# A graph network's second layer: the last three stores of a pass as single transfers of 125 partitions

## The chip, the cores and the metric

The kernel runs on one core of a Trainium2 chip. The metric is the time of the whole program in microseconds of device time, the median of several executions. TensorE (PE) multiplies matrices into PSUM banks, VectorE (DVE), ScalarE (ACT) and GpSimd (POOL) work elementwise, and SyncE (SP) issues most of the transfers between the on-chip memory (SBUF) and the device memory. The transfers themselves are carried out by 16 DMA engines.

## What is computed

Four graph layers follow one another on a table of 10,000 nodes with 512 features; each adds its result to its input and normalises every row. The change touches the second layer only, a fixed-point iteration over 2,500 edges sorted by target:

```
step(out):  Ax  = segment_sum(sup[:, None] * out[edge_col], edge_row)
            out = (x * b + (Ax + out) * a) / denom
x = layernorm(x + scan(step, x, length=10))
```

An edge has a weight `sup`, a source `edge_col` and a target `edge_row`. Each of the ten iterations needs the rows of the previous one at every edge's source.

## The kernel before

Nodes without an edge need no iteration, so the kernel keeps only one row per edge in sorted order: `E` = 2,500 rows in `ET` = 20 tiles of `P` = 125 rows (one row of 512 floats, 2,048 bytes, per partition). A target whose edges lie in two neighbouring tiles has its row in one of `NM` = 20 extra shared rows, `EM`. The values of the iteration lie in the SBUF tile `Y[125, 20, 512]` (in the first pass in `CR`).

The ten iterations are written as a first one without a table and nine passes i = 1 to 9 of the same shape. A pass goes through a table in device memory, because every edge needs the row of an arbitrary other edge:

- SP (`sp_L1`, lines 1195 to 1206) writes `Y` to the table `Yd[i % 2]` (`y_table` in the trace). `Y_STORES` (line 1396) cuts the 20 tiles into seven stores: tiles 0-3, 4-7, 8-11, 12-15, then 16-17, 18 and 19. Each waits on the semaphore `P_out` for its last tile. `store_tiles` (line 1182) makes two transfers of a store: one of the partitions 0 to 111 (`HI` = 112, line 1185) and one of the 13 partitions 112 to 124 (line 1186). After the seven stores the shared rows follow, one transfer of 20 rows (line 1201), once DVE has them (`M_rows`).
- All 15 transfers of a pass raise one semaphore, `y_put`. `Y_PUT` (line 1397) is what a pass adds to it.
- POOL (`pool_L1`) waits until `y_put` holds everything of the pass (line 1422) and then issues 20 indirect transfers, one per tile, that gather the rows into `V1` (line 1424).
- PE (`pe_L1`) multiplies each gathered tile t with the tile's weights `Ss` into bank t mod 5 (line 1473, waits for gather t), and once per four tiles adds to the sums of the shared rows (line 1438). After the last tile it forms the shared rows (line 1491).
- DVE (`dve_L1`, line 1633) turns bank t into `Y[:, t, :]` and raises `P_out`; at the end it makes the shared rows (line 1642, raises `M_rows`). ACT (line 1525) writes the constant part of the next pass into the bank that came free.

So one pass is a ring: gathers, products, rows, stores, and then the next pass's gathers, which may read any row and therefore wait for all the stores. The order of the stores on SP's queue is the order of the code.

Of the kernel before, what the change touches and what calls it, by code (L numbers as in the profile page):

```python
# [5 lines left out]
P = 125  # L6
# [35 lines left out]
def gnn_kernel(nc, x, x_cols, cols, rows, b1_row, wsmall, w32, w_ffn, w_left, ident_in, w_r1, w_r2, w_l1, w_l2, w_q, w_k, w_v, w_o,  # L42
               keys, key_cols, rec_in, earlier_in, mask_in, abs_in, out):
    ctx = ExitStack()
    with ctx:
# [3 lines left out]
        def sem(name):  # L49
            return ctx.enter_context(nc.semaphore(name))  # L50
# [13 lines left out]
        def at(off, shape, parts=128, dt=F32):  # L64

            n = 1
            for v in shape:
                n *= v
            assert off + n <= AR, (off, shape)
            ap = arena[0:parts, off:off + n]  # L70
            if dt != F32:
                ap = ap.bitcast(dt)
            if len(shape) == 2:
                ap = ap.rearrange("p (a b) -> p a b", b=shape[1])
            return ap
# [650 lines left out]
        Yd = [nc.dram_tensor(f"y_table{q}", (E + NM, D), F32).ap() for q in range(2)]  # L726
# [216 lines left out]
        def store(sp, table, base, g, rows4, s):  # L943

            dst = grp(table[base:base + E, :], g)
            sp.dma_start(dst[0:HI], rows4[0:HI]).then_inc(s, 16)
            sp.dma_start(dst[HI:P], rows4[HI:P]).then_inc(s, 16)

        def load(sp, rows4, table, base, g, s):
            src = grp(table[base:base + E, :], g)  # L950
            sp.dma_start(rows4[0:HI], src[0:HI]).then_inc(s.s, 16)
            sp.dma_start(rows4[HI:P], src[HI:P]).then_inc(s.s, 16)
# [229 lines left out]
        def store_tiles(sp, table, t0, t1, rows, s):  # L1182

            dst = table[t0 * P:t1 * P, :].rearrange("(t p) d -> p t d", p=P)
            sp.dma_start(dst[0:HI], rows[0:HI, t0:t1, :]).then_inc(s, 16)
            sp.dma_start(dst[HI:P], rows[HI:P, t0:t1, :]).then_inc(s, 16)

        def sp_L1(sp, c):
            for g in range(EG):
                c.y += TG  # L1190
                sp.wait_ge(L_y, c.y)
                store_tiles(sp, X1s, g * TG, (g + 1) * TG, Y, x1s_put)
            sp.dma_start(EM[:, :], Y[P - 1:P, :, :]).then_inc(m_in, 16)

            def step(i, par):
                first = isinstance(i, int) and i == 1
                for t0, t1 in Y_STORES:
                    sp.wait_ge(P_out, t1 if first else i * ET + (t1 - ET))
                    store_tiles(sp, Yd[par], t0, t1, CR if first else Y, y_put)
                sp.wait_ge(M_rows, i)  # L1200
                sp.dma_start(Yd[par][E:E + NM, :], EM[:, :]).then_inc(y_put, 16)
            step(1, 1)
            with sp.Fori(1, ITERS // 2) as h:
                step(h * 2, 0)
                step(h * 2 + 1, 1)
            for g in range(EG):
                sp.wait_ge(P_cr, ET * (ITERS - 2) + TG * (g + 1))
                if g == 0:
                    sp.wait_ge(x1s_put, 32 * EG)
                load(sp, CR[:, g * TG:(g + 1) * TG, :], X1s, 0, g, e1_f[g])  # L1210
            sp.wait_ge(*e1_f[EG - 1].full(32))
            for g in range(EG):
                sp.wait_ge(*e1_f[g].full(32))
            sp.wait_ge(M_rows, ITERS)
            sp.dma_start(CRM[:, :], CR[P - 1:P, :, :]).then_inc(m_in, 16)
            sp.wait_ge(P_out, ET * ITERS)
            for dst, src in ((WQ, w_q), (WK, w_k), (WV, w_v), (WO, w_o)):
                sp.dma_start(dst, src).then_inc(w2_in, 16)
            for g in range(EG):
                c.y += TG  # L1220
                sp.wait_ge(L_y, c.y)
                store(sp, X2d, 0, g, Y[:, g * TG:(g + 1) * TG, :], x2_put)
            sp.wait_ge(xm_rdy, 1)
            sp.dma_start(X2d[2 * E:2 * E + NM, :], EM[:, :]).then_inc(x2_put, 16)
            sp.wait_ge(x2_put, X2_ALL)
# [142 lines left out]
        V1, Y, CR = at(6312, [ET, D], P), at(16552, [ET, D], P), at(26792, [ET, D], P)  # L1368
# [3 lines left out]
        y_put = sem("y_put")  # L1372
# [21 lines left out]
        x1s_put, m_in = sem("x1_by_src_put"), sem("shared_rows_in")  # L1394
        m_pre, xm_rdy, m_sc, m_rt = sem("shared_before_sums"), sem("shared_x2"), sem("shared_var"), sem("shared_root")
        Y_STORES = [(0, 4), (4, 8), (8, 12), (12, 16), (16, 18), (18, 19), (19, 20)]
        Y_PUT = 32 * len(Y_STORES) + 16
        X2_ALL = 2 * 32 * EG + 16
        RING1 = 5

        def pool_L1(pool, c):
# [19 lines left out]
            for i in range(1, ITERS):  # L1421
                pool.wait_ge(y_put, i * Y_PUT)
                for t in range(ET):
# [110 lines left out]
        def dve_L1(dve, c):  # L1534
# [90 lines left out]
            def step(i):  # L1625
                dve.wait_ge(y_put, i * Y_PUT)
                nc.vector.scalar_tensor_tensor(EM, EM, RRM[:, 0:1], CRM, ALU.mult, ALU.add).then_inc(m_pre, 1)

                before = CR if isinstance(i, int) and i == 1 else Y

                def own(t):
                    dve.wait_ge(P_sum, i * ET + (t + 1))
                    nc.vector.scalar_tensor_tensor(Y[:, t, :], before[:, t, :], RR[:, t:t + 1], bank[t % RING1][0:P, :],  # L1633
                                                   ALU.mult, ALU.add).then_inc(P_out, 1)
                for t in range(ET - 1):
                    own(t)
                dve.wait_ge(M_ps, i + 1)
                nc.vector.tensor_copy(MB, bank[7][:, :]).then_inc(M_sb, 1)
                own(ET - 1)
                dve.wait_ge(m_pre, i)  # L1640
                dve.wait_ge(M_ps2, i + 1)
                nc.vector.scalar_tensor_tensor(EM, bank[5][0:NM, :], RRM[:, 0:1], EM, ALU.mult,
                                               ALU.add).then_inc(M_rows, 1)
# [1107 lines left out]
```

## Time and profile before

| | us |
|---|---|
| Median of 3 runs (3117.52 to 3121.24) | 3119.29 |
| The profiled execution's own time | 3123.35 |
| Its span, first to last instruction | 3121.5 |
| Idle time of POOL that the stores' landing ended, over 9 passes | 110.5 |
| First and last gather issue of the nine passes (`y_table`), from the span's start | 1624.2 and 2003.7 |

The span is one execution as the hardware profiler saw it. An engine's busy time says little by itself here; what counts is which wait ends last at each turn of the ring. SP's transfers appear in a timeline at the moment SP issues them, with the time the issue took; when the data moves is seen in the share of time for which the 16 DMA engines carry packets, where one engine that is always busy counts 1/16 = 0.06. A transfer's landing is seen in who waited for it.

### The profile page before, as it was taken

To read this page: it belongs to the slowest core of one execution; us is meant where nothing else is said; L and a number is where in the kernel's file an instruction comes from. 1 tells how busy PE (TensorE), PEld (TensorE's weight loads), DVE (VectorE), ACT (ScalarE), POOL (GpSimd) and SP (SyncE) were. 2 spreads that over 40 slices of the span, in tenths; PEclk is the share of its full clock that TensorE was granted. 3 is DMA by queue.
4 is the path that set the end of the run, shared out by engine and by line. 5 is a ranking of instruction groups with operands and counts; after the bars stand their busy time and mean duration, and the time that the engine had idled before them with its cause. 6 is when DMAs were issued, how large, how long until landed. Compare 5 with 4: busy or idle time off the path is not lost.

```text
span 3121.5 us, 29317 instructions
## 1 busy us (share of the span) xinstructions
PE 2388.7 (77%) x9340; PEld 1248.1 (40%) x9340; DVE 1899.9 (61%) x3792; ACT 1300.8 (42%) x1935; POOL 1164.3 (37%) x850
## 2 busy tenths in 40 slices
PE   5779999999998448987066766539888777568877
PEld 2445555555555324543021111124443643235455
DVE  3378989889899741235753434545556547737663
ACT  2898888888874311120422322201110012145544
POOL 1354553644648434310625565420220202133322
PEclk8899999999999679999578878769888588779989
DMA  6224333333332144316725545740120101132212
GB/s 200 79 71 119 96 102 117 96 114 108 103 114 73 43 120 136 91 56 184 198 82 153 159 124 151 192 123 0 54 60 18 40 18 48 40 86 69 71 45 56
DMA packets 212498, 297.37 MB, mean 95 GB/s; under 512 B 98571, under 2 KB 98941, under 8 KB 210998
## 3 DMA queue, kind: packets, MB, share of 16 engines
q1 hardware_dynamic: 107436, 213.12, 22.8%
q0 software_dynamic: 104960, 82.99, 10.6%
q8 instruction: 53, 0.87, 0.1%
q14 instruction: 49, 0.39, 0.0%
HBM read 170.88 MB, written 160.48 MB: 106 GB/s over the span
## 4 chain that ended last, share of the span: by engine, by line
PE 39%; DVE 21%; issue 11%; ACT 10%; POOL 9%; DMA 7%; SPq 2%; DVEq 0%; POOLq 0%; ACTq 0%
PE bank L1823 7%; PE bank L847 6%; POOL arena L939 5%; POOL arena L1424 5%; ACT RD L414 3%; PE bank L2249 3%; DVE st L525 3%; PE bank L827 2%; PE bank L289 2%; DMA arena<-y_table,ids 2%; PE bank L290 2%; ACT arena L855 2%; PE bank L2132 2%; ACT arena L467 2%; PE bank L801 1%
## 5 line engine op out<-in xcount | busy, mean ns | idle before, releaser
L939 POOL DMA_INDIRECT arena<-x_table,idd x120 | 156.3, 1303 | 697.7 <-DVE arena L905 317.9
L282 PE MATMUL bank<-arena 128*125 128x512 f32 x640 | 290.4, 608 | 41.0 <-DMA arena<-x_cols 23.1
L847 PE MATMUL bank<-arena 128*125 128x512 f32 x640 | 283.5, 601 | 8.9 <-DVE arena L1343 7.0
L1424 POOL DMA_INDIRECT arena<-y_table,ids x180 | 229.1, 1273 | 162.6 <-DMA y_table<-arena 110.5
L298 PE MATMUL bank<-arena 128*125 128x512 f32 x640 | 278.8, 593 | 1.3 <-ACT arena L391 1.3
L659 POOL TENSOR_TENSOR arena<-arena,rowv 125x512 f32<-125x512 f32 x80 | 106.8, 1367 | 461.7 <-PE bank L290 167.1
L1473 PE MATMUL bank<-arena 125*125 125x512 f32 x360 | 206.2, 705 | 91.5 <-DMA arena<-y_table,ids 88.5
L1633 DVE SCALAR_TENSOR_TENSOR arena<-arena,v,bank 125x512 f32<-125x512 f32 x180 | 134.5, 747 | 202.3 <-PE bank L1473 193.8
L855 ACT ACTIVATE arena<-bank 128x500 f32<-128x500 f32 (+1 forms) x210 | 116.5, 590 | 322.9 <-PE bank L827 233.2
L1525 ACT ACTIVATE bank<-arena 125x512 f32<-125x512 f32 x180 | 107.9, 601 | 283.3 <-DVE arena L1633 278.3
L801 PE MATMUL bank<-ident,arena 125*128 125x125 f32 x640 | 101.8, 326 | 158.6 <-DMA arena<-x_table,idd 106.3
L1823 PE MATMUL bank<-arena 128*125 128x512 f32 x480 | 213.8, 608 | 3.8 <-ACT arena L855 3.8
L861 ACT ACTIVATE lsr<-lsr 125x4 f32<-125x4 f32 (+1 forms) x55 | 11.2, 204 | 480.6 <-DVE lsr L894 448.6
L282 PEld LDWEIGHTS bank<-arena 128*125 128x125 f32 x640 | 119.9, 192 | 197.0 <-issue 171.7
L847 PEld LDWEIGHTS bank<-arena 128*125 128x125 f32 x640 | 120.4, 191 | 161.1 <-issue 149.8
L298 PEld LDWEIGHTS bank<-arena 128*125 128x125 f32 x640 | 120.2, 188 | 154.2 <-issue 154.0
L801 PEld LDWEIGHTS bank<-ident,arena 125*128 125x128 f32 x640 | 93.6, 186 | 181.0 <-issue 104.5
L855 ACT ACTIVATE arena<-bank,colv 128x500 f32<-128x500 f32 (+1 forms) x105 | 70.6, 709 | 220.4 <-PE bank L801 129.9
L1473 PEld LDWEIGHTS bank<-arena 125*125 125x125 f32 x360 | 68.0, 213 | 230.5 <-issue 173.7
L661 POOL TENSOR_SCALAR arena<-arena,q 125x512 f32<-125x512 f32 x80 | 159.2, 2003 | 0.0
L391 ACT ACTIVATE arena<-bank,colv 128x500 f32<-128x500 f32 x220 | 139.5, 713 | 35.8 <-PE bank L290 34.6
L274 PE MATMUL bank<-ident,arena 125*128 125x125 f32 x960 | 125.2, 286 | 36.3 <-ACT arena L476 28.1
(390 smaller groups left out, 4997.7 us busy)
## 6 DMA issues: line engine op xcount, KB each, us to landing
y_table<-arena SPq DMA_DIRECT2D x36, 896.0 KB
p_table<-arena SPq DMA_DIRECT2D x25, 896.0 KB
z_table<-arena SPq DMA_DIRECT2D x25, 896.0 KB
x_table<-arena SPq DMA_DIRECT2D x25, 896.0 KB
arena<-x_cols SPq DMA_DIRECT2D x20, 1000.0 KB, 6.1
arena<-x SPq DMA_DIRECT2D x20, 896.0 KB
out<-arena SPq DMA_DIRECT2D x20, 896.0 KB
x_by_src<-arena SPq DMA_DIRECT2D x5, 896.0 KB
```

Of the source, the lines that this page charges most:

```text
L282: i = nc.tensor.matmul(b[0:P, :], xT[:, k, j * P:(j + 1) * P], W1r[:, k, :], start=k == 0, stop=k == KC - 1)
L298: i = nc.tensor.matmul(b[0:P, :], hT[:, k, j * P:(j + 1) * P], W2r[:, k, :], start=k == 0, stop=k == KC - 1)
L391: nc.scalar.activation(dst, st_.bank(part, i)[0:parts, 0:GR], func, **kw).then_inc(NT_sb, 1)
L661: nc.gpsimd.tensor_scalar(T[1 - par][:, j, :], T[1 - par][:, j, :], q2[1 - par][:, j:j + 1], None, ALU.mult).then_inc(B["wq"], 1)
L801: i = nc.tensor.transpose(b[:, j * P:(j + 1) * P], src, ident[0:P, 0:P])
L847: i = nc.tensor.matmul(b[0:P, 0:n], fT[:, k, j * P:(j + 1) * P], W[:, k, :], start=q * KC + k == 0, stop=q * KC + k == last)
L855: nc.scalar.activation(dst, bank[(c.t - 1) % 4][0:src_rows, 0:n], func, **kw).then_inc(T_sb, 1)
L939: nc.gpsimd.indirect_dma_start(out=dst, out_offset=None, in_=table, in_offset=bass.IndirectOffsetOnAxis(ap=idx, axis=0), bounds_check=limi ...
L1424: nc.gpsimd.indirect_dma_start(out=V1[0:P, t, :], out_offset=None, in_=Yd[i % 2], in_offset=bass.IndirectOffsetOnAxis(ap=ids[:, 2, t:t + 1 ...
L1473: nc.tensor.matmul(bank[t % RING1][0:P, :], Ss[:, t, :], V1[:, t, :], start=False, stop=True, skip_group_check=True).then_inc(P_sum, 1)
L1633: nc.vector.scalar_tensor_tensor(Y[:, t, :], before[:, t, :], RR[:, t:t + 1], bank[t % RING1][0:P, :], ALU.mult, ALU.add).then_inc(P_out, 1)
L1823: i = nc.tensor.matmul(b[0:P, :], fT[:, k, j * P:(j + 1) * P], W[:, k, :], start=k == 0, stop=k == KC - 1)
```

## The change

The first four stores of a pass stay pairs of 112 and 13 partitions. The last three (tiles 16-17, tile 18, tile 19) become one transfer of all 125 partitions each, issued from line 1203 of the changed kernel. The sum that `y_put` reaches in a pass is adapted: 12 transfers instead of 15.

```diff
-                    store_tiles(sp, Yd[par], t0, t1, CR if first else Y, y_put)
+                    rows = CR if first else Y
+                    if t1 - t0 > 2:
+                        store_tiles(sp, Yd[par], t0, t1, rows, y_put)
+                    else:
+                        sp.dma_start(Yd[par][t0 * P:t1 * P, :].rearrange("(t p) d -> p t d", p=P),
+                                     rows[0:P, t0:t1, :]).then_inc(y_put, 16)
...
-        Y_PUT = 32 * len(Y_STORES) + 16
+        Y_PUT = sum(32 if t1 - t0 > 2 else 16 for t0, t1 in Y_STORES) + 16
```

On SP's queue the end of a pass in the loop reads as follows before the change; `y_table` is the table, `arena` the SBUF region that holds `Y` and the shared rows, and the sizes are partitions x (tiles x) elements:

```order
L1185 DMA y_table<-arena 112x2x512
L1186 DMA y_table<-arena 13x2x512
L1198 REGISTER_ALU
L1185 DMA y_table<-arena 112x512
L1186 DMA y_table<-arena 13x512
L1185 DMA y_table<-arena 112x512
L1186 DMA y_table<-arena 13x512
L1201 DMA y_table<-arena 20x512
```

And so after it:

```order
L1203 DMA y_table<-arena 125x2x512
L1198 REGISTER_ALU
L1203 DMA y_table<-arena 125x512 x2
L1206 DMA y_table<-arena 20x512
```

Three transfers of 13 partitions are gone from each pass, nothing changes place, and the other engines' instructions are the same.

## Rows read from the trace of the kernel before

**Rows 1.** The chain that ended last, from 1620 to 2010 us, by line:
```profile
by line: POOL arena L1424 36.2%; issue 30.2%; DMA arena<-y_table,ids 15.7%; PE bank L1473 5.6%; DMA y_table<-arena 4.3%; PE bank L1438 3.0%; PE bank L1491 1.7%; DVE arena L1642 1.2%; POOLq L1424 0.9%; SPq L1186 0.5%; SPq L1185 0.5%; DVE are
```

**Rows 2.** A wait of POOL, 1620 to 2010 us: total us, times, longest us:
```profile
POOL arena L1424 <- DMA y_table<-arena: 110.5, 9, 15.2
```

**Rows 3.** Last chain again, single pieces (start, us, what), four of nine:
```profile
1621.81 1.47 DMA y_table<-arena
...
1753.44 1.51 DMA y_table<-arena
...
1927.95 1.77 DMA y_table<-arena
...
1970.02 2.83 DMA y_table<-arena
```

**Rows 4.** Timeline, end of pass 8 (start, us, engine, line, operation):
```profile
1920.22 0.31 SPq L1185 DMA_DIRECT2D y_table<-arena  x1
...
1924.02 0.31 SPq L1185 DMA_DIRECT2D y_table<-arena  x1
...
1926.92 0.31 SPq L1185 DMA_DIRECT2D y_table<-arena  x1
...
1927.95 0.27 SPq L1201 DMA_DIRECT2D y_table<-arena  x1
...
1930.62 1.27 POOL L1424 DMA_INDIRECT arena<-y_table,ids  x1 [10.97 <-DMA y_table<-arena]
```

**Rows 5.** Timeline of SP, loads of 125 partitions at the program's start:
```profile
30.64 0.57 SPq L2544 DMA_DIRECT2D Sd<-keys  x1
31.26 4.60 SPq L2544 DMA_DIRECT2D Md<-keys  x1
```

**Rows 6.** Windows while these loads run; last two columns DMA share and GB/s:
```profile
24.00:28.00 4.00, 3.31 (x19) 2.00 (x19) 0.00 (x0) 1.51 (x3) 0.00 (x0) 1.00 1.06 214
...
36.00:40.00 4.00, 4.00 (x11) 1.70 (x10) 1.88 (x3) 0.00 (x0) 2.76 (x3) 1.00 0.32 117
40.00:44.00 4.00, 3.58 (x9) 1.29 (x7) 1.00 (x2) 0.00 (x0) 1.52 (x2) 1.00 0.33 132
```

**Rows 7.** Windows in passes 5, 2 and 8: length, engines busy, PEclk, DMA share, GB/s:
```profile
1800.00:1800.50 0.50, 0.00 (x0) 0.00 (x0) 0.00 (x0) 0.00 (x0) 0.00 (x0) 1.00 0.00 0
1800.50:1801.00 0.50, 0.00 (x0) 0.00 (x0) 0.00 (x0) 0.00 (x0) 0.00 (x0) 1.00 0.35 82
...
1660.00:1661.00 1.00, 1.00 (x9) 0.29 (x2) 0.72 (x2) 0.74 (x2) 0.00 (x0) 1.00 0.91 260
...
1921.00:1931.00 10.00, 4.99 (x16) 1.24 (x16) 4.47 (x7) 2.40 (x4) 0.39 (x1) 1.00 0.67 216
```

**Rows 8.** The page's DMA queue of SP (packets, MB, share of 16 engines):
```profile
q1 hardware_dynamic: 107436, 213.12, 22.8%
```

**Rows 9.** Timeline of SP, shared rows' store in pass 5:
```profile
1799.90 0.27 SPq L1201 DMA_DIRECT2D y_table<-arena  x1
```

**Rows 10.** Timeline of SP, end of pass 4, the stores of tiles 16-17 and 19:
```profile
1745.58 0.31 SPq L1185 DMA_DIRECT2D y_table<-arena  x1
...
1752.41 0.31 SPq L1185 DMA_DIRECT2D y_table<-arena  x1
```

**Rows 11.** Timeline of SP, store of tiles 16-17 in pass 1:
```profile
1615.51 0.30 SPq L1185 DMA_DIRECT2D y_table<-arena  x1
```

**Rows 12.** Timeline, end of pass 6, from the store of tiles 16-17 on:
```profile
1837.60 2.12 SPq L1186 DMA_DIRECT2D y_table<-arena  x1
...
1841.17 0.74 DVE L1642 SCALAR_TENSOR_TENSOR arena<-bank,arena 20x512 f32<-20x512 f32 x1 [0.29 <-PE bank L1491]
...
1842.61 0.33 SPq L1201 DMA_DIRECT2D y_table<-arena  x1
```

**Rows 13.** Last chain, end of pass 8: the piece of the last gathers:
```profile
1915.21 6.75 DMA arena<-y_table,ids
```

## The prediction, made before the changed kernel ran

> **What bounds the kernel now.** I read first the chain that ended last, cut to the stretch of the second layer's loop. It is made of the gathers' issues on POOL and the pauses between them, then of the landing of the last gathers, the last products, and the landing of the stores [rows 1]. PE, the busiest engine of the page, is a guest here. Then the waits of POOL: its only real wait in the loop is for the stores of `y_table`, nine times, once a pass, 110.5 us in all [rows 2]. So a pass is: 20 gathers issued one after the other, the last one lands, the last rows are made, the last stores land, the next pass begins. Whatever moves the moment at which all stores of a pass have landed moves everything behind it by the same amount, nine times; no other work can hide it, since every gather waits for it.
>
> The third view is that moment itself. The chain's pieces show how long the last transfer (the 20 shared rows) took from issue to landing: 1.47 to 1.51 us in passes 1, 3, 4 and 5, and 1.76 to 2.83 us in passes 2, 6, 7, 8 and 9 [rows 3]. The first group finds an idle queue; in the second the transfer stands behind stores that are still being carried out. In pass 8 it was issued at 1927.95 and landed at 1929.7, and the next pass's first gather began at 1930.62 [rows 4]. So in five passes of nine the DMA engines are already the last thing to finish, and the question is what the change does to the queue in front of them.
>
> **The change, part by part.** (1) *Removed:* three issues of 13 partitions a pass on SP. (2) *Changed:* three transfers of 112 partitions become transfers of 125. The bytes are the same: 250, 125 and 125 rows of 2,048 bytes.
>
> What the second part costs depends on how many DMA engines a transfer of 125 partitions uses. No such store is in the trace, but loads of that shape are: from 31 us on SP has only transfers of 125 partitions under way [rows 5], and the DMA share falls from 1.06 to a plateau of 0.32 to 0.33 [rows 6]. 5/16 is 0.31. I read that as five engines busy and eleven idle. Stores cut at 112 reach a share of 0.91 [rows 7], all sixteen.
>
> The Trainium skill says the same from the other side ("DMA: Bandwidth & Descriptors", section "Why a DMA increments its semaphore by 16 and not by 1"): a transfer takes the largest number of engines up to 16 that divides its slowest dimension, which makes 16 of 112, 13 of 13 and 5 of 125; and on this path they are the lowest-numbered ones. The plateau agrees. The same page's section "Rules for kernel authors" speaks for the change: two transfers to disjoint halves of the partitions are no use, one should take a single transfer. By that rule the sum would be the second rival's.
>
> So per engine: before, a tile is 7 rows on each of 16 engines and one more on 13 of them, 8 at most. Now it is 25 rows on each of five. The three stores put 2x8 + 8 + 8 = 32 rows on an engine before and 50 + 25 + 25 = 100 after.
>
> *Time of a row.* Loads on five engines: 132 GB/s at a share of 0.33, 25 GB/s an engine, 0.082 us for 2,048 bytes [rows 6]. Stores on sixteen, beside gathers: 260 GB/s at 0.91, 17.9 GB/s an engine, 0.115 us [rows 7]. The average of SP's queue over the program is 0.228 x 16 x 3121.5 / 107436 = 0.106 us a packet [rows 8]. The new stores run on five engines, like the loads, but they are stores of shorter rows (the loads bring 2,500 numbers to a partition), partly beside gathers. I take **0.095 us**, a little nearer to the loads, and keep 0.082 and 0.115 as ends.
>
> *Start and landing.* The shared rows of pass 5 were issued at 1799.90 into an idle queue [rows 9]; up to 1800.5 nothing moved, then all did [rows 7]. I take 0.85 us from issue to first row. With 1.47 us in all for a similar one [rows 3] and 2 rows an engine, 0.4 us remain for the landing.
>
> *A pass with a full queue (pass 8)* [rows 4]. Tiles 12-15 are issued at 1920.22; 28 + 4 rows an engine at 0.106 us after 0.85 us end at 1924.5. Tiles 16-17 are issued at 1924.02, so data starts at 1924.9, and 50 rows last until 1929.6. Tile 18 (issued by then) ends at 1932.0, tile 19 at 1934.4, the shared rows at 1934.6, landed at 1935.0. Before it was 1927.95 + 1.77 = 1929.72. **+5.2 us**, and 26 for the five passes of this kind.
>
> *A pass in which tile 19 comes late (pass 4)* [rows 10]. Tiles 16-17 start at 1746.4, end at 1751.2; tile 18 ends at 1753.6; tile 19, issued at 1752.41, stands behind it and ends at 1755.9; shared rows landed at 1756.5, against 1753.44 + 1.51 = 1754.95. +1.6. The same working gives +1.3 for pass 3 and +0.5 for pass 5, where the gap in front of tile 19 is longest: 3.4 together.
>
> *Pass 1* stores one after the other what lies ready, with 6.3 us from the issue of tiles 16-17 to that of the shared rows [rows 3, 11]: 1616.4 + 102 x 0.095 + 0.4 = 1626.5, against 1623.3. +3.2.
>
> *The removed issues* are worth something only where SP is late. The shared rows are ready at 1841.91 in pass 6 and issued at 1842.61, 0.7 us late, because SP had stood 2.12 us at a 13-partition transfer [rows 12]; pass 9 looks the same, with the longest landing of all, 2.83 us [rows 3]. That gain is counted at nothing: the transfer that would be issued sooner then waits behind 100 rows on its engines. I also count nothing for the wait of SP at the larger transfers: it stood 4.6 us at them at the start [rows 5], but only while their engines had work queued, and those engines set the end.
>
> **Sum:** 26 + 3.4 + 3.2 = 32.6 us. Against the profiled execution (3123.35 us, of which 3121.5 span) that is 3156.0; that execution is 4.1 us above the median of the runs, so the forecast for the median is 3119.3 + 32.6 = **3152 us**. With 0.082 us a row a full pass costs 5.2 - 102 x 0.013 = 3.9 us, pass 1 costs 1.9 and the three others some 1 together, 22 us in all; with 0.115 it is 7.2 x 5 + 5.2 + 9 = 50 us. That gives 3141 to 3169.
>
> **The rivals.**
> - *Five engines, but not always the same five.* If each transfer took other engines, the 100 rows would not queue on one. Tile 19 of pass 8 would end at 1926.92 + 0.85 + 2.4 = 1930.2, landed at 1930.6, +0.9; nine times that is 8 us: 3127. For it: the plateau of 0.32 shows one share, not which engines. Against: consecutive loads on different engines would overlap and lift the share over 0.31, and it stayed there for 8 us [rows 6].
> - *The other side: 125 partitions spread evenly.* Then each transfer is as fast as the pair, 8 rows an engine, and SP has three issues less. SP's stop of 2.12 us in pass 6 [rows 12], and the like in pass 9, shrinks, which brings tiles 18 and 19 out up to 1.5 us earlier there and 0.3 us in the three other full passes: -4 us, 3115. It decides if the new transfers' share in a pass's tail is near that of before. Against it stands the plateau, unless it came from the loads' other side, keys that all partitions read alike. To come out over 6.2 us faster, it would also have to bring the last gathers in sooner.
> - *More than the queue.* The last gathers already take 6.75 us to land [rows 13], and some of their rows share the five loaded engines, now for 5 us a pass instead of 2; and PE stands idle longer, so its granted clock, 1.00 (2.4 GHz) in those windows of pass 5 [rows 7], may be 1.2 GHz for more of the products. One to two microseconds a pass, +12: 3164.
>
> **How the numbers follow.** Forecast 0.66, more than the queue 0.13, not the same five 0.11, spread evenly 0.10. The range is to hold the first two, and the ends of the row time: down to 3135, a little under the 3141 of the cheapest row, because the drain of tiles 12-15 may be shorter than taken, and up to 3171. A run can tell 0.2%, 6.2 us, from no change. Slower by more than that are the first three cases, 0.89 with a little of the third falling under it; same 0.09; faster 0.03.
>
> **What would show it.** In the tail of a full pass the DMA share falls from 0.67 over ten us [rows 7] to some 0.4, and to 0.3 once only the new transfers are left, for about 5 us after SP's last issue. The chain's piece from the shared rows' issue to the landing grows from 1.8 to some 7 us in passes 2, 6, 7, 8 and 9, and to 2 to 3 us in 3 to 5. POOL's nine waits grow from 110.5 to some 143 us; its 180 issues and the gathers keep their durations. I am wrong if the share in the tail stays near 0.7 (spread evenly), or if it is 0.6 for half the time (different engines), or if POOL's wait grows by clearly less than the total.

## The result

| | before | changed |
|---|---|---|
| Median of 4 runs, us | 3120.26 | 3178.17 |
| Lowest and highest | 3117.52, 3127.41 | 3166.11, 3187.08 |
| Span of the profiled execution | 3121.5 | 3185.3 |

The changed kernel takes 1.0189 times as long, interval 1.0164 to 1.0214: 58 us more. The direction was as forecast; the forecast of 3152 us was 26 us too low and the time lies 7 us above the range of 3135 to 3171. One execution of an experiment's kernel (tiles 12 to 17 as one store) took 5021.87 us; it counts as slow and is left out of that run's ratio.

### The profile page after: what moved, and what is told of

The parts are those of the page before. It is cut to its first block, busy times and chain, and to the rows that moved or that the text cites. A ratio compares the mean times of both kernels' runs of the same rounds, so it can differ in the third digit from the quotient of the medians.

```text
span 3185.3 us, 29290 instructions
## 1 busy us (share of the span) xinstructions
PE 2394.6 (75%) x9340; PEld 1252.1 (39%) x9340; DVE 1900.7 (60%) x3792; ACT 1301.3 (41%) x1935; POOL 1166.2 (37%) x850
## 4 chain that ended last, share of the span: by engine, by line
PE 38%; DVE 21%; issue 11%; ACT 10%; DMA 9%; POOL 9%; SPq 2%; DVEq 0%; POOLq 0%; ACTq 0%
PE bank L1828 7%; PE bank L847 6%; POOL arena L1429 4%; POOL arena L939 4%; ACT RD L414 3%; PE bank L2254 3%; DMA y_table<-arena 3%; DVE st L525 3%; PE bank L289 2%; PE bank L827 2%; DMA arena<-y_table,ids 2%; PE bank L290 2%; PE bank L2137 2%; ACT arena L855 2%; PE bank L801 2%
## 5 line engine op out<-in xcount | busy, mean ns | idle before, releaser
L1478 PE MATMUL bank<-arena 125*125 125x512 f32 x360 | 208.8, 712 | 156.2 <-DMA arena<-y_table,ids 153.7
L1429 POOL DMA_INDIRECT arena<-y_table,ids x180 | 229.6, 1275 | 224.2 <-DMA y_table<-arena 172.1
```

The source lines that it names most:

```text
L1429: nc.gpsimd.indirect_dma_start(out=V1[0:P, t, :], out_offset=None, in_=Yd[i % 2], in_offset=bass.IndirectOffsetOnAxis(ap=ids[:, 2, t:t + 1 ...
L1478: nc.tensor.matmul(bank[t % RING1][0:P, :], Ss[:, t, :], V1[:, t, :], start=False, stop=True, skip_group_check=True).then_inc(P_sum, 1)
```

## The profile after

Lines are renumbered: the gathers are at line 1429, the stores of 125 partitions at 1203, the shared rows at 1206. POOL's wait, from 1620 to 2100 us (us in total, times, longest), answers [rows 2]:

```profile
POOL arena L1429 <- DMA y_table<-arena: 172.1, 9, 21.0
POOL arena L1429 <- issue: 52.1, 171, 0.3
```

The wait for the stores grew from 110.5 to 172.1 us, by 61.6 of the 63.8 us that the span grew. The issues' pauses are the same 52.1. So the time went where the forecast put it. The chain that ended last shows the landings of the shared rows one by one (start of the issue, us until landed). All nine after the change:

```profile
1626.15 5.14 DMA y_table<-arena
...
1672.49 11.19 DMA y_table<-arena
...
1724.19 10.95 DMA y_table<-arena
...
1775.54 10.79 DMA y_table<-arena
...
1827.18 10.83 DMA y_table<-arena
...
1878.51 8.37 DMA y_table<-arena
...
1931.27 5.03 DMA y_table<-arena
...
1977.58 9.71 DMA y_table<-arena
...
2028.35 10.83 DMA y_table<-arena
```

And the five of the kernel before that [rows 3] leaves out, passes 2, 3, 5, 6 and 7:

```profile
1663.54 1.98 DMA y_table<-arena
...
1709.03 1.51 DMA y_table<-arena
...
1799.90 1.47 DMA y_table<-arena
...
1842.61 2.60 DMA y_table<-arena
...
1885.74 1.76 DMA y_table<-arena
```

1.5 to 2.8 us became 5 to 11 us. From one landing to the next is one pass. In the kernel before, passes 2, 6, 7, 8 and 9 take 42.2 to 43.8 us, and passes 3, 4 and 5 take 44.4 to 46.4. After the change seven passes take 48.9 to 52.4 us, and pass 7 takes 49.4. The end of pass 2 in the timeline, the counterpart of [rows 4]:

```profile
1666.18 0.31 SPq L1185 DMA_DIRECT2D y_table<-arena  x1
...
1667.90 4.54 SPq L1203 DMA_DIRECT2D y_table<-arena  x3
...
1670.03 0.75 DVE L1638 SCALAR_TENSOR_TENSOR arena<-arena,v,bank 125x512 f32<-125x512 f32 x1 [0.33 <-PE bank L1478]
...
1672.49 1.49 SPq L1206 DMA_DIRECT2D y_table<-arena  x1
1683.70 0.74 DVE L1632 SCALAR_TENSOR_TENSOR arena<-arena 20x512 f32<-20x512 f32 x1 [11.90 <-DMA y_table<-arena]
1684.58 1.28 POOL L1429 DMA_INDIRECT arena<-y_table,ids  x1 [21.02 <-DMA y_table<-arena]
```

And the DMA engines meanwhile (columns as in [rows 7]: PEclk, DMA share, GB/s last):

```profile
1667.00:1677.00 10.00, 3.96 (x15) 0.68 (x13) 3.69 (x6) 2.40 (x4) 0.00 (x0) 0.89 0.56 167
...
1671.00:1681.00 10.00, 0.00 (x0) 0.00 (x0) 0.74 (x1) 0.42 (x1) 0.00 (x0) 0.69 0.32 98
...
1672.00:1674.00 2.00, 0.00 (x0) 0.00 (x0) 0.00 (x0) 0.00 (x0) 0.00 (x0) 1.00 0.32 102
1674.00:1676.00 2.00, 0.00 (x0) 0.00 (x0) 0.00 (x0) 0.00 (x0) 0.00 (x0) 0.72 0.47 118
1676.00:1678.00 2.00, 0.00 (x0) 0.00 (x0) 0.00 (x0) 0.00 (x0) 0.00 (x0) 0.50 0.31 98
1678.00:1680.00 2.00, 0.00 (x0) 0.00 (x0) 0.00 (x0) 0.00 (x0) 0.00 (x0) 0.50 0.31 113
1680.00:1682.00 2.00, 0.00 (x0) 0.00 (x0) 0.00 (x0) 0.00 (x0) 0.00 (x0) 0.50 0.08 30
1682.00:1683.50 1.50, 0.00 (x0) 0.00 (x0) 0.00 (x0) 0.00 (x0) 0.00 (x0) 0.50 0.06 22
```

The plateau at 0.31 to 0.32 is there: five engines of sixteen, from 1672 to 1680, while no other engine of the core works. The one window at 0.47 is when the shared rows move, a transfer that uses ten engines by the divisor rule; that they go out there is read from the share alone. [rows 7] has 0.67 and 216 GB/s in pass 8 of the kernel before, in a stretch that begins 0.8 us after the issue of tiles 12-15. The stretch that begins there in this pass, from 1667, has 0.56 and 167 GB/s, and the one from 1671 has 0.32 and 98.

Two things were not in the forecast. The five engines move 98 to 113 GB/s, 20 to 23 GB/s each, where the forecast read 25 from the loads [rows 6]. And from 1680 on the share is 0.08, then 0.06, which is 1/16: one engine is alone for some 3 us, while the four others have finished. It is not slower than they are at that time. In the trace's packet records its last 25 rows of tile 19 begin at 1681.15, end at 1683.15 and start 0.080 us apart, and the two shared rows follow until 1683.32; the others had ended by 1680.59. So it stands a whole tile behind by then, and lost that time earlier in the pass. In passes 3, 4 and 5 the last engine ends 2.0 to 2.6 us after the next to last, in pass 6, the shortest of the seven long ones, 0.4 us after it.

## Experiments

All times are medians, beside the kernel before on the same chip, with the ratio to it and its interval; the chip is not the same for all experiments, so they are compared by their ratios. "Rows" are the 2,048-byte rows that the most loaded DMA engine carries in a pass's three last stores and the shared rows: 34 before, 102 in the changed kernel, by the divisor rule (see the forecast).

### Another cut of the pairs

Four kernels keep pairs and 15 transfers a pass, and move only the cut of the last three stores.

```diff
-                    store_tiles(sp, Yd[par], t0, t1, CR if first else Y, y_put)
+                    store_tiles(sp, Yd[par], t0, t1, CR if first else Y, y_put, 120 if t1 - t0 <= 2 else HI)
```

(`store_tiles` takes the cut as its last argument; 100, 115 and 124 likewise.)

**120 and 5 partitions.** 

> The last three stores of a pass are pairs again, but of 120 and 5 partitions. Queue theory (what counts is the number of rows on the most loaded DMA engine, at about 0.127 us a row, as the tails of the changed kernel's passes show: 102 rows between the drain of tiles 12-15 and the landing took some 13 us): 120 spreads over 15 engines (8 rows each), 5 over five (1 row), so 9 rows a tile instead of 8, about 4 rows a pass more: 0 to +5 us against the kernel before. Rival, size theory (any transfer of more than 112 partitions is slow, because it leaves the 16-engine split, whatever the count of engines): most of the +58 us. Rival, issue theory (a single transfer holds SP for longer than a pair, and that delays what follows): 0, as there are pairs.

3121.32 us, ratio 1.0005 (0.9982 to 1.0028). No difference. A transfer of 120 partitions, more than 112, is not slow as such: the size theory is out.

**100 and 25 partitions.** 

> The last three stores of a pass are pairs of 100 and 25 partitions. Queue theory: 100 spreads over ten engines (10 rows each) and 25 over five (5 rows), so 15 rows a tile on the most loaded engines, 62 rows in the tail of a pass instead of 34. 28 rows at 0.127 us are 3.6 us a pass, +25 to +32 us. Issue theory: pairs as before, -1 to +3 us.

3136.82 against 3119.29 us, ratio 1.0065 (1.0041 to 1.009), +20 us by the ratio. Same number of transfers, same bytes, only more rows on some engines. The queue theory has the sign; its +25 to +32 lies above the median, and the interval (+13 to +28 us) reaches its lower end.

**115 and 10 partitions.** 

> The last three stores are pairs of 115 and 10 partitions. 115 spreads over five engines (23 rows each), 10 over ten (1 row): 24 rows a tile, 98 in the tail of a pass, on the same five engines as in the changed kernel, but in 15 transfers a pass as before. Queue theory: within 5 us of the changed kernel, +50 to +58 us. Issue theory (the single transfer, not its spread, costs): like the kernel before, 0. Alignment theory (in the changed kernel one of the five engines lags because of where its 25 partitions begin): the lagging engine, alone for 2 us and more at the end of half of the passes, is gone, +35 to +45 us.

3164.65 against 3115.32 us, ratio 1.0151 (1.0117 to 1.0184), +47 us. This is the decisive run: 15 transfers in pairs as before, and most of the cost of the change, because 115 has the divisor 5 and no larger one under 16. The issue theory is out. The alignment theory expected the lagging engine to be gone; in pass 4 one engine is again alone at the end:

```profile
1771.00:1773.00 2.00, 0.00 (x0) 0.00 (x0) 0.00 (x0) 0.00 (x0) 0.00 (x0) 0.50 0.38 124
1773.00:1775.00 2.00, 0.00 (x0) 0.00 (x0) 0.00 (x0) 0.00 (x0) 0.00 (x0) 0.50 0.07 29
```

**124 and 1 partition.** 

> The last three stores are pairs of 124 and 1 partition: 124 spreads over four engines (31 rows each), 1 goes to one engine: 32 rows a tile, 130 in the tail instead of 34. Queue theory, with the 0.13 us a row and pass that the runs with 17 and 34 rows more gave: 96 x 0.13 = 12.5 us a pass in full passes, +85 to +110 us against the kernel before, clearly more than the changed kernel's +58. Issue theory: 0. Size theory (over 112 partitions is slow as such): as the changed kernel, +58.

3189.5 against 3115.32 us, ratio 1.0246 (1.0211 to 1.0281), +77 us: more than the changed kernel, as only the queue theory says, a little under its numbers. The share in pass 2's tail, after SP's last issue, is 0.26 to 0.27, four engines of sixteen:

```profile
1671.00:1673.00 2.00, 0.00 (x0) 0.00 (x0) 0.00 (x0) 0.00 (x0) 0.00 (x0) 0.64 0.27 99
1673.00:1675.00 2.00, 0.00 (x0) 0.00 (x0) 0.00 (x0) 0.00 (x0) 0.00 (x0) 0.50 0.26 102
```

### One part of the change alone

```diff
-                    if t1 - t0 > 2:
+                    if not (t0 == 19):
```

(against the changed kernel; the other two have `t0 == 16` and `t0 == 18`, and `Y_PUT` is adapted.)

**Only tile 19.** 

> Only tile 19, the last store, is one transfer of 125 partitions; tiles 16-17 and 18 stay pairs of 112 and 13. Queue theory: 17 rows more on the most loaded engines, 2.2 us in each of nine passes, whether tile 19 is late or not, since nothing comes after it but the shared rows: +15 to +20 us. Issue theory: a third of the 58 us or less, and little where SP has nothing queued; +0 to +5 us in passes in which tile 19 comes late.

3139.07 us, ratio 1.0071 (1.0046 to 1.0096), +22 us.

**Only tiles 16-17.** 

> Only tiles 16-17 go as one transfer of 125 partitions; tiles 18 and 19 stay pairs. Queue theory: 50 rows instead of 16, 34 more a pass; in a pass whose tail is full (tile 19 within 3 us of tile 18) they stand in front of what follows: 4.3 us, in a pass in which tile 19 comes 6 us late they are gone by then: about 0. With five to nine full passes +22 to +39 us. Issue theory: a third of the 58 us, +19 us, alike in all passes.

3143.99 us, ratio 1.0106 (1.0077 to 1.0135), +33 us by the ratio, +25 by the medians.

**Only tile 18.** 

> Only tile 18 goes as one transfer of 125 partitions. Together with the runs in which only tile 19 (+20 us) and only tiles 16-17 (+25 to +33 us) do, a queue is additive: 58 - 20 - 25 to 33 leaves +5 to +13 us; 17 rows at 0.085 us in nine passes are +13 us, less where the gap before tile 19 lets the queue drain. A rival in which the three transfers only cost together (SP stopped at the third) has 0 here.

3134.51 against 3119.49 us, ratio 1.0055 (1.0039 to 1.0071), +17 us, more than expected. The three parts give 22 + 33 + 17 = 72 us by ratios, where the whole has 55 to 59, and 20 + 25 + 15 = 60 by medians, where the whole has 53 to 58. They add up, or to a little more than the whole; nothing costs only in company.

### The changed kernel again, single transfers, and all seven stores

**The changed kernel.** 

> The changed kernel itself once more, beside the others of this call and the kernel before on the same chip. Queue theory at the slope that the pairs of 100, 115 and 124 partitions gave (0.08 to 0.09 us for each row more on the most loaded engine and pass, times nine passes): 68 rows x 9 x 0.085 = +52 us; measured before: +58. If it is again above +55, single transfers cost something beside their rows.

3172.88 against 3119.49 us, ratio 1.0177 (1.0162 to 1.0193), +55 us. This execution's profile differs from the first one's in a way that matters for the forecast. Six of its nine landings:

```profile
1623.85 5.06 DMA y_table<-arena
...
1668.12 7.88 DMA y_table<-arena
...
1719.21 4.39 DMA y_table<-arena
...
1766.81 3.86 DMA y_table<-arena
...
1811.39 10.39 DMA y_table<-arena
...
2012.93 4.80 DMA y_table<-arena
```

and the other three, passes 6 to 8:

```profile
1862.16 10.14 DMA y_table<-arena
...
1912.30 9.97 DMA y_table<-arena
...
1961.69 8.02 DMA y_table<-arena
```

Passes 3, 4 and 9 have short landings here, 3.9 to 4.8 us; in the first profile only pass 7 was. These are the passes in which tile 19 comes 5.6 to 6.9 us after tile 18, so that part of the queue has drained. Which passes are of this kind is not a property of the kernel but changes from execution to execution. The time differs too: this profile's span is 3161.7 us, the first one's 3185.3. But not all of that is the mix, since passes 2 and 8 are short here (47.1 and 47.4 us) with tile 19 only 2.2 us behind tile 18.

**Single transfers of 115.** Tiles 16-17, 18 and 19 as one transfer of 115 partitions each, the rest of the four tiles as one transfer of 10 partitions (`Y_PUT` is adapted):

```diff
+                    if t0 < 16:
+                        store_tiles(sp, Yd[par], t0, t1, rows, y_put)
+                    else:
+                        sp.dma_start(Yd[par][t0 * P:t1 * P, :].rearrange("(t p) d -> p t d", p=P)[0:115],
+                                     rows[0:115, t0:t1, :]).then_inc(y_put, 16)
+                    if t1 == ET:
+                        sp.dma_start(Yd[par][16 * P:ET * P, :].rearrange("(t p) d -> p t d", p=P)[115:P],
+                                     rows[115:P, 16:ET, :]).then_inc(y_put, 16)
```

> Tiles 16-17, 18 and 19 each go as one transfer of 115 partitions (five engines, 23 rows a tile), and partitions 115 to 124 of the four tiles follow as one transfer: the rows of the run with pairs of 115 and 10, 98 on the most loaded engine, but single transfers where they count. Theory that only rows count: as that run, +49 us (+45 to +53). Theory that single transfers in a row cost something of their own, or let SP run further ahead: as the changed kernel, +55 or more.

3160.1 against 3119.49 us, ratio 1.0143 (1.011 to 1.0177), +45 us. The same as the pairs of 115 and 10 (+47) within the intervals (+34 to +55 us here): that a transfer is single costs nothing that these runs show.

**Single transfers of 112**, the same edit with 112 in place of 115: 

> Tiles 16-17, 18 and 19 each go as one transfer of 112 partitions, and the 13 partitions of all four tiles follow as one transfer: 13 issues a pass instead of 15, all sixteen engines used, the same rows. Issue theory (fewer issues on SP are worth something, as the spread-evenly rival had it): -2 to -6 us. Queue theory: rows on the most loaded engine are the same, and the last transfer now carries 4 rows behind tile 19 instead of 1, 0.3 us a pass: -2 to +3 us.

3118.45 against 3115.32 us, ratio 1.0013 (0.9996 to 1.003). The interval is -1 to +9 us, so the gain of 2 to 6 us that the issue theory promised for two issues less is excluded for this edit as a whole. The edit also puts three more rows behind tile 19, which the expectation priced at 0.3 us a pass, 2.7 us in all; a gain of up to 4 us from the issues beside that cost is not excluded.

**All seven stores as single transfers of 125.** 

> All seven stores of a pass are single transfers of 125 partitions: 500 rows a pass on each of five engines. The first four stores lie beside the gathers, whose issues take 31 us a pass. If that cover held, the cost would be that of the changed kernel, +58 us. But 500 rows at 0.1 us are 50 us, longer than the whole pass (42 to 44 us), and the first store starts 12 us into it: the last row lands at the earliest 12 + 50 us after the first gather, so a pass takes some 63 to 75 us instead of 42 to 44: +170 to +280 us.

3276.62 against 3119.49 us, ratio 1.0495 (1.0477 to 1.0514), +154 us. Only 54 us follow from the last three, 100 from four stores that lie beside the gathers. With 400 rows on each of five engines the gathers no longer cover them. The expected pass length, 63 us at least, is what the trace shows: passes 2 to 9 take 60 to 67 us from first gather to first gather, 63.2 on average against 43.7 before, which is 156 us in eight passes. The expected total of +170 us and more was too high. Here, too, the last rows come later: from a pass's first gather to DVE's row of tile 19 it takes 41.0 to 43.5 us, in the long-landing passes before 37.1 to 38.6. SP's seven issues of pass 3 lie between 1703.96 and the shared rows. The merged row runs from the first issue to the last and holds SP's waits for the rows; singly the last three take 6.69, 5.68 and 3.17 us, the others 1.34 us or less:

```profile
1679.58 1.58 SPq L1206 DMA_DIRECT2D y_table<-arena  x1
1703.96 41.06 SPq L1203 DMA_DIRECT2D y_table<-arena  x7
...
1745.07 4.35 SPq L1206 DMA_DIRECT2D y_table<-arena  x1
```

### Two attempts at the gap before tile 19

**Tiles 12 to 17 as one store**, `(12, 18)` in place of `(12, 16), (16, 18)` in `Y_STORES`, with pairs: 

> Tiles 12-15 and 16-17 go as one store (pairs of 112 and 13 partitions), issued when tile 17 is ready. Theory on the passes in which tile 19 comes late: there the store of tiles 12-15 starts within 1 us of the last gather and shares the engines with it; without it at that time, the gap of 4 to 8 us between the rows of tiles 18 and 19 is gone in all passes (first gather to tile 19: 38.5 us instead of 41 to 42), -3 us in each of the three or so passes that have it; against that up to 1 us a pass more of queue at the end: -8 to +3 us. Rival (the gap has another cause, the queue at the end is all that counts): gaps stay, 0 to +8 us.

3135.93 against 3115.32 us, ratio 1.0059 (1.0035 to 1.0083), +18 us: missed. The gap between tiles 18 and 19 is gone in all passes, as expected (2.2 us at most in the rows of DVE). What was not thought of is SP's queue. In pass 3 of this kernel:

```profile
1702.53 0.31 SPq L1185 DMA_DIRECT2D y_table<-arena  x1
1702.88 1.48 SPq L1186 DMA_DIRECT2D y_table<-arena  x1
1704.47 1.58 SPq L1185 DMA_DIRECT2D y_table<-arena  x1
1706.09 2.18 SPq L1186 DMA_DIRECT2D y_table<-arena  x1
1708.32 0.52 SPq L1185 DMA_DIRECT2D y_table<-arena  x1
```

Behind the larger transfer SP stands 1.5 to 2.2 us at each of the next three issues, and what follows goes out later: the shared rows are issued 3.3 to 4.1 us after DVE has made tile 19, in the kernel before it was 1.1 us in five of eight passes and at most 2.3. In the changed kernel SP stands too (1.05 us at tile 18, 1.63 at tile 19, 1.49 at the shared rows in pass 2; the 4.54 us above also hold waits for rows), but the engines set the end there.

**The store of tiles 12-15 one tile later**, with pairs:

```diff
-                    sp.wait_ge(P_out, t1 if first else i * ET + (t1 - ET))
+                    due = t1 + 1 if t1 == 16 else t1
+                    sp.wait_ge(P_out, due if first else i * ET + (due - ET))
```

> The kernel before, with one wait moved: the store of tiles 12-15 goes out when tile 16 is ready, not tile 15 (in the passes in which tile 19 comes late that is 2.5 us later, in the others 0.9 us). Theory that this store, when it starts beside the last gathers, makes gather 19 late: the passes with a gap of 6 to 8 us between the rows of tiles 18 and 19 (44.4 to 46.4 us long) become full ones (42.2 to 43.8 us), about -2.5 us in each of the three or so that have it, against up to 0.5 us more queue in the others: -6 to 0 us. Rival, the gap comes from the gathers themselves: gaps stay, 0 to +4 us.

3124.69 against 3117.77 us, ratio 1.0013 (0.9998 to 1.0027). The gaps are gone here too, and nothing is won (-1 to +8 us, where the theory had -6 to 0): DVE waits 32.9 us in all for the shared rows to land, before it was 19.4, so the queue at the end of a pass is longer.

That the store of tiles 12-15 makes the gap is supported by this, not shown: in these two kernels and the next one no pass of the three profiles has it, but neither has any pass of the profiles of two kernels in which that store was not moved (only tile 19, and the pairs of 115 and 10).

**The same wait with the three transfers of 125:** 

> The changed kernel with the same moved wait. If every pass is full now, the difference to the run with the moved wait and pairs is the change's cost in full passes alone: with 0.095 us a row and the forecast's working +5.2 us a pass, +45 us in all; with 0.12 us a row 8 us a pass, +70 us. Against the changed kernel itself: 0 to +10 us, as its passes in which tile 19 comes late are gone.

3199.43 us, ratio 1.0247 (1.0223 to 1.0271). Against the run with pairs that is 74.7 us, 8.3 us in each of nine passes, all of them full. The landings of the shared rows in the two kernels, passes 2 and 3, first with pairs:

```profile
1678.94 2.67 DMA y_table<-arena
1722.30 2.96 DMA y_table<-arena
```

and with transfers of 125:

```profile
1677.57 10.47 DMA y_table<-arena
1728.35 10.16 DMA y_table<-arena
```

So with this wait moved, 68 more rows on the most loaded engine cost 8.3 us a pass. The forecast had 5.2 for a pass with a full queue.

## The forecast, point by point

**What bounds the kernel: right.** POOL's wait for the stores took 61.6 of the 63.8 us.

**Five engines, always the same: right.** The share in the tail is 0.31 to 0.32 where only those transfers run, with a cut at 124 it is 0.26 to 0.27, and the time goes with the largest divisor up to 16 of the partition count. Cost against rows on the most loaded engine, each by its ratio:

| rows | 34 | 38 | 51 (18) | 51 (19) | 62 | 68 (16-17) | 98 | 98 single | 102 | 130 |
|---|---|---|---|---|---|---|---|---|---|---|
| us | 0 | +2 | +17 | +22 | +20 | +33 | +47 | +45 | +55, +59 | +77 |

From 34 rows to 130 that is 77 / (96 x 9) = 0.089 us a row. The three partial changes lie 3 to 8 us above that line, which is not explained. If other engines had been used for each transfer, the rival's +8 us would have come out, and the parts would not have added up. The Trainium skill's rule on the number of engines ("DMA: Bandwidth & Descriptors", section "Why a DMA increments its semaphore by 16 and not by 1") agrees with the shares read for 125 and 124 partitions and with the times of the other cuts; with 115 the share never shows those transfers alone (0.35 to 0.49 in pass 2, beside the ten engines of the small transfers). The other rule weighed, in the same page's "Rules for kernel authors", that two transfers to disjoint halves of the partitions are no use, would have given the spread-evenly rival; the page has one transfer of 128 partitions in their place, and here, with 125, the pair of 112 and 13 beats the single one by 1.8 to 1.9%.

**The time of a row, and with it the +5.2 us of a full pass: the step that failed, first part.** The forecast took 0.095 us, with 0.082 and 0.115 as ends. By its own working, pass 2 of the first profile has the queue of tiles 12-15 end at 1666.18 + 0.85 + 3.4 = 1670.4 and the last row at 1683.7 - 0.4 = 1683.3: 12.9 us for 102 rows, 0.126 us, outside both ends. While five engines are busy a row takes 2,048 / (20 to 23) = 0.09 to 0.10 us, near the value taken; the rest is the 3 us in which one engine is alone. The sum assumed that five engines with 25 rows a tile end together, and they don't. Against the long-landing passes of the kernel before (42.7 us on average), those of the changed kernel take 8.5 us more in the first profile and 6.5 in the second, and with the moved wait the difference was 8.3.

**The kinds of passes: the same step, second part.** The forecast read three passes of the one trace as cheap (+1.1 us each) and took that for a property of the kernel. Before, such passes take 45.3 us on average; in the second profile three of them take 47.6, +2.3 us each, and in the first profile one takes 49.4, +4.1. Where such a pass turns into one with a full queue, it costs 51.2 - 45.3 = 5.9 us.

With these numbers both profiles add up against the profile of before. The second has the mix that the forecast took: 5 x 6.5 + 3 x 2.3 + 3.6 in pass 1 = 43 us, and POOL's wait is 153.3 - 110.5 = 42.8 us longer; the forecast for it was 32.6. The first has 5 x 8.5 + 2 x 5.9 + 4.1 + 3.7 = 62 us, and the wait 61.6. So of the 29 us that the forecast is short of in the first profile, some 16 lie in the five full passes and some 12 in the three that it had as cheap. The medians, +55 and +58, lie between the two profiles; which mix the other executions had is not known, nor why the full passes cost 6.5 us in one and 8.5 in the other.

**Pass 1: right.** +3.2 forecast. From the issue of tiles 16-17 to the landing of the shared rows it took 7.8 us before (1615.51 to 1621.81 + 1.47) [rows 3, 11]; now it is 1619.86 to 1626.15 + 5.14, 11.4 us: +3.7.

```profile
1619.86 2.02 SPq L1203 DMA_DIRECT2D y_table<-arena  x3
```

**Removed issues counted at nothing: right.** Single transfers of 112, with their remainder behind tile 19, gain nothing (1.0013), and single ones of 115 cost what pairs cost. A gain of a few us under the cost of that remainder is not excluded.

**The rival "more than the queue".** Its time, 3164, was nearer than the forecast's, but its mechanism was hardly seen. In the passes with a full queue it takes 37.1 to 38.6 us from the first gather to DVE's row of tile 19 before, 38.5 to 39.1 in the first profile of the changed kernel and 37.2 to 38.8 in the second; that is half a microsecond a pass in one profile and nothing in the other, not one to two. The granted clock did fall to 0.50 (1.2 GHz) during the longer pause, where no engine works; it shows in the windows above. The tile products of all nine passes together kept PE busy for 208.8 us, 206.2 before, so the clock cannot have cost much; no run priced it by itself.

**The range.** It was built from the row time's ends alone. The mix of passes varied with the execution and was left out. By the forecast's own terms a cheap pass that turns full costs 7.8 us instead of 1.1 (5.2, and 2.6 by which it was shorter), so two of them add 13 us: with the upper end of the row time, 3169, that would have reached some 3182.

## What to carry to other kernels

Count rows per DMA engine, not bytes or transfers: a transfer whose partition count has no large divisor up to 16 (125, 115, 124) piles its rows on few engines, and here a second small transfer for the remainder cost nothing that the runs show. The DMA share shows the number of engines where only that transfer runs, a plateau at k/16. Read a size that depends on how passes fall in time from more than one execution before it goes into a sum.

## What the runs showed of the hardware

- Transfers of 125 partitions run on five of sixteen engines and of 124 on four (share 0.31 and 0.26), for 2,048-byte rows from SBUF to device memory at 20 to 23 GB/s an engine on five and 25 on four. Those of 115 cost what five engines would make them cost. Not expected: one of the five finishes 2.0 to 2.7 us after the others in four passes of the first profile, and 0.4 and 0.5 us in two more; with 23 rows a tile it was 2.1 us in pass 4. Once it is alone, a row takes 0.080 us, so it is not slow then; why it fell behind is open.
- SP's issue of a transfer takes 0.25 to 0.46 us with little queued, up to 2.65 us behind stores that are still being carried out, and up to 7.1 us where all seven are single transfers of 125. What exactly it waits for was not tried.
- In some passes tile 19 comes 6 to 8 us after tile 18, in others 2 us. With the store of tiles 12-15 started one or two tiles later no such gap was left in three profiles, and no kernel gained by it, since SP's queue or the engines' at the end grew instead. That this store is the cause is likely and not shown.
